# Growing the key matrix M with three products a head instead of four: two over all 128 rows with the high keys, and one for each head over 64 rows with the low keys

## The chip, the cores and the metric

The kernel runs on one core of one Trainium2 chip. The metric is the device time of one execution in microseconds (us). TensorE is PE in the profile, its weight loads PEld, VectorE DVE, ScalarE ACT, GpSimd POOL, and SyncE, which issues the DMAs, SP.

## The reference

A cross attention and a quantised linear layer, each behind a layer norm and each added to its input:

```python
def xattn(q, latent_kv, Wq, Wkv_expand, Wout):      # q: (8, 1024, 1024), latent_kv: (8, 64, 256)
    qp = q @ Wq.T
    k, v = jnp.split(latent_kv @ Wkv_expand.T, 2, axis=-1)
    # 16 heads of 64 columns: qh, kh, vh
    scores = jnp.einsum('bhqd,bhkd->bhqk', qh, kh) / jnp.sqrt(64)
    scores = jnp.where(causal, scores, jnp.finfo(scores.dtype).min)
    out = jnp.einsum('bhqk,bhkd->bhqd', softmax(scores), vh)
    return out.reshape(b, sq, H) @ Wout.T

def ffn(x, weight):                                  # weight: (1024, 1024)
    w_fp8, w_scale = quant_e4m3(weight)              # one scale for the whole tensor
    x_fp8, x_scale = quant_e4m3(x)
    return ((x_fp8 @ w_fp8.T) * (x_scale * w_scale)).astype(bfloat16)

x = x + xattn(layernorm(x), ctx, Wq, Wkv_expand, Wout)
x = x + ffn(layernorm(x), w)
```

## The kernel before

**The algebra.** There are only 64 keys a batch, so the kernel never forms the queries. For each batch it makes M, whose 64 columns for head h are Wq of that head times that head's keys, and N, which is the values times Wout. The scores of a tile of 128 rows are then x times M (1024 by 1024, 16 heads by 64 keys), and the attention's output is the probabilities times N. Each of these products is done in float16 with every number split in a high and a low part: `PASSES` lists the three part products (high by high, high by low, low by high), and `split_product` runs them over the 8 chunks of 128 rows: 8 times 3 times 2 halves of 512 columns, 48 matmuls a tile (L636).

**The order of the work.** 64 tiles, 8 a batch, 8 batches. The PE program is written out by hand: `step(b, tt, e, t)` issues the scores S of tile t+1 and then the output O of tile t. M of the next batch is grown in the seventh step of a batch (`tt == TB - 2`): two of its 8 blocks are put between chunks of S (`KEYS_AT_S`) and six between chunks of O (`KEYS_AT_O`). The N blocks are grown in pairs in the last step of a batch and in the first of the next (`make_n_pair`, L623), with matmuls on 64 rows and 64 columns of the array. The M of batch 0 is grown ahead of the first tile, each block followed by the turning of a piece of Wout (`turn_wout`, L728).

**The part that is changed.** `make_m(ct, n)` grows one block of 128 rows of M into 1024 columns of PSUM (`grow_ps`, two such buffers). `wq_stack` holds for each head, in 64 of the partitions, the high part of its weight, and in the other 64 the low part: even heads have the high part in partitions 0 to 63 (`EVEN`), odd heads in 64 to 127 (`ODD`). `k_hilo` holds the keys' high part beside the weight's high part and the low part beside the low, `k_lohi` the other way round. So two matmuls of 128 rows and 64 columns a head (L609 and L610) give all four part products, 32 matmuls a block. `place(h)` is the column block of head h in M, and so in the scores and probabilities. ACT rounds the block to its high part (`take_m`, L862) and DVE makes the low part and frees the buffer (`take_m`, L1099). `load_k` (L375) brings the keys of a batch from `kv_dram` in 8 DMAs on SP's queue, issued by `next_k` in the first step of the batch before. `got_k` counts them.

Of the kernel before, what the change touches and what calls it, by code (L numbers as in the profile page):

```python
# [25 lines left out]
F16 = mybir.dt.float16  # L26
BF16 = mybir.dt.bfloat16
U32 = mybir.dt.uint32
ALU = mybir.AluOpType
ACT = mybir.ActivationFunctionType  # L30
# [3 lines left out]
P = 128  # L34
# [7 lines left out]
N_SCALE = 2.0 ** -14  # L42
# [13 lines left out]
def xattn_ffn_kernel(nc, x, ctx, Wq, Wkv, Wout, Wffn, out):  # L56
    B, S, H = x.shape
    SK, L = ctx.shape[1:]
    NH = H // HD
    NP = NH // 2  # L60
# [11 lines left out]
    with ExitStack() as scope:  # L72
        def sb(name, shape, dt):
            return scope.enter_context(nc.sbuf_tensor(name, shape, dt))
# [9 lines left out]
        wq_stack = sb("wq_stack", [P, NH, H], F16)  # L84
        wo_t = sb("wo_t", [P, 2, NP, H], F16)
        m_buf = sb("m_buf", [P, 2, CT, H], F16)
        n_buf = sb("n_buf", [P, 2, NP, H], F16)
        k_hilo = sb("k_hilo", [P, NH, SK], F16)
        k_lohi = sb("k_lohi", [P, NH, SK], F16)
        v_rows = sb("v_rows", [P, 2, NP, SK], F16)  # L90

        w8_raw = sb("w8_raw", [P, CT, H], BF16)
# [21 lines left out]
        pt_buf = [halves(i) for i in (10, 11)]  # L114
# [39 lines left out]
        ps_s, ps_o, ps_x, ps_p = (ps_all[:, i * H:(i + 1) * H] for i in range(4))  # L154
# [20 lines left out]
        EVEN, ODD = slice(0, HD), slice(HD, P)  # L175
# [28 lines left out]
        got_k = sem("got_k")  # L204
# [19 lines left out]
        o_full = sem("o_full")  # L224
# [83 lines left out]
        QUAD = CT // 2  # L308
        grow_ps = [ps_p, ps_x]
# [9 lines left out]


        def place(h):
            return h // 4 * 4 + (0, 2, 1, 3)[h % 4]

        FIRST_PAIRS_AT = {0: 0, 3: 1, 6: 2, 8: 3}
        PAIRS_AT = {0: 1, 5: 2, 8: 3}
# [4 lines left out]
        block = scope.enter_context(nc.Block())  # L330
# [16 lines left out]
        def _(sp):  # L347
# [21 lines left out]

            def load_k(of):  # L370

                for to, swap in ((k_hilo, 0), (k_lohi, 1)):
                    for s, rows in enumerate((EVEN, ODD)):
                        for e in range(2):
                            sp.dma_start(to[rows].rearrange("d (j e) k -> d e j k", e=2)[:, e],  # L375
                                         of(s ^ swap, e)).then_inc(got_k, 16)

            def load_v(of):
                for s in range(2):
# [118 lines left out]
            for k in range(2):  # L498
                cols = slice((1 - k) * HALF, (2 - k) * HALF)
# [52 lines left out]
        def _(pe):  # L552
# [12 lines left out]
            to = next_slot()  # L565
            for lt in range(LT):
                for a in range(KEYS // P):
                    mm = nc.tensor.transpose(to[:, (lt * 4 + a) * P:(lt * 4 + a + 1) * P],
                                             ctx_f[:, a, lt * P:(lt + 1) * P], ident[:])
# [32 lines left out]
            def make_m(ct, n):  # L602
                to = grow_ps[ct % 2]
                if not is_step(n, 0):
                    pe.wait_ge(grow_free[ct % 2], n)
                for h in range(NH):
                    cols = to[:, place(h) * SK:(place(h) + 1) * SK]
                    w = wq_stack[:, h, ct * P:(ct + 1) * P]
                    nc.tensor.matmul(cols, w, k_hilo[:, h, :], start=True, stop=False)  # L609
                    mm = nc.tensor.matmul(cols, w, k_lohi[:, h, :], start=False, stop=True)  # L610
                mm.then_inc(grow_full[ct % 2], 1)


# [13 lines left out]
                                    mm.then_inc(grow_full[k], 1)  # L627


            def split_product(to, left, right, full, weave=lambda c: None, ready=lambda c: None):  # L630
                for c in range(CT):
                    ready(c)
                    for i, (ls, rs) in enumerate(PASSES):
                        for half in range(2):
                            cols = slice(half * HALF, (half + 1) * HALF)
                            mm = nc.tensor.matmul(to[:, cols], left[:, ls, c * P:(c + 1) * P], right[:, rs, c, cols],  # L636
                                                  start=(c == 0 and i == 0),
                                                  stop=(c == CT - 1 and i == len(PASSES) - 1))
                    if c == CT - 1:
                        mm.then_inc(full, 1)  # L640
                    weave(c + 1)
# [14 lines left out]
            def step(b, tt, e, t):  # L656
                known = isinstance(t, int)
                last = known and t >= T - TB
                n_here = is_step(tt, 0)
                if n_here:  # L660
                    pe.wait_ge(got_v, 32 * b + 32)
                if not known or t + 1 < T:
                    m_last = is_step(tt, TB - 1)
                    m_next = is_step(tt, TB - 2) and not last
                    pe.wait_ge(x_turned, 16 * t + 32)
                    pe.wait_ge(s_read, t + 1)
                    if m_next:
                        pe.wait_ge(got_k, 128 * b + 256)
                        if b == 2:
                            pe.wait_ge(w_scale_made, 1)  # L670
                        if b >= 3:
                            pe.wait_ge(w8_ready, 2 * (b - 2))

                    def between(c):
                        if n_here:
                            m = (FIRST_PAIRS_AT if t == 0 else PAIRS_AT).get(c)
                            if m is not None:
                                make_n_pair(b, m)
                        if m_next and c in KEYS_AT_S:
                            make_m(KEYS_AT_S[c], uses(b + 1, 0, KEYS_AT_S[c]))  # L680

                    def m_chunk(c):
                        if m_last:
                            pe.wait_ge(grow_free[c % 2], uses(b + 1, 0, c) + 1)

                    between(0)
                    split_product(ps_s, xt_buf[1 - e], m_buf, s_full, between, m_chunk)
                if last and 1 <= tt <= 4:
                    turn_w8(tt - 1)
                if b == 2 and is_step(tt, 5):  # L690
                    pe.wait_ge(w_amax_rows, 1)
                    nc.tensor.transpose(ps_x[:, 0:P], w_spread, ident[:]).then_inc(w_amax_turned, 1)
                pe.wait_ge(p_turned, 16 * t + 16)
                pe.wait_ge(x1_ready, t + 1)
                if is_step(tt, TB - 2) and not last:
                    def next_m(c):
                        for k in KEYS_AT_O.get(c, ()):
                            make_m(k, uses(b + 1, 0, k))

                    split_product(ps_o, pt_buf[e], n_buf, o_full, next_m)  # L700
                elif known and t == T - 1:
                    for half in range(2):
                        cols = slice(half * HALF, (half + 1) * HALF)
                        for c in range(CT):
                            for i, (ls, rs) in enumerate(PASSES):
                                mm = nc.tensor.matmul(ps_o[:, cols], pt_buf[e][:, ls, c * P:(c + 1) * P],  # L706
                                                      n_buf[:, rs, c, cols], start=(c == 0 and i == 0),
                                                      stop=(c == CT - 1 and i == len(PASSES) - 1))
                        mm.then_inc((o_half, o_full)[half], 1)
                else:  # L710
                    def n_chunk(c):
                        if n_here:
                            pe.wait_ge(grow_free[c % 2], uses(b, 1, c) + 1)

                    def next_n(c):
                        if is_step(tt, TB - 1) and c == NEXT_PAIR_AT:
                            pe.wait_ge(got_v, 32 * b + 64)
                            make_n_pair(b + 1, 0)

                    split_product(ps_o, pt_buf[e], n_buf, o_full, next_n, n_chunk)  # L720


            def turn_wout(j):
# [8 lines left out]
            for i in range(2):  # L732
                pe.wait_ge(got_wout[i], 16)
            turn_wout(0)
            pe.wait_ge(got_k, 128)
            for i in range(4):
                pe.wait_ge(wq_moved[i], 64)
            for c in range(CT):
# [69 lines left out]
        def _(act):  # L808
# [45 lines left out]

            def take_n(c, n):
                act.wait_ge(grow_full[c % 2], n + 1)
                nc.scalar.activation(n_buf[:, 0, c, :], grow_ps[c % 2][:], ACT.Copy,  # L857
                                     scale=N_SCALE).then_inc(grow_hi[c % 2], 1)

            def take_m(c, n):  # L860
# [165 lines left out]
            for k in range(2):  # L1026
                cols = slice((1 - k) * HALF, (2 - k) * HALF)
# [6 lines left out]
        def _(dve):  # L1034
# [45 lines left out]
            for i in range(2):  # L1080
# [3 lines left out]
                                                    in1=k_hi_t[:, part, :], op0=ALU.mult, op1=ALU.subtract)  # L1084
# [5 lines left out]

            def take_n(c, n):
                dve.wait_ge(grow_hi[c % 2], n + 1)
                nc.vector.scalar_tensor_tensor(out=n_buf[:, 1, c, :], in0=grow_ps[c % 2][:], scalar=N_SCALE,  # L1093
                                               in1=n_buf[:, 0, c, :], op0=ALU.mult,
                                               op1=ALU.subtract).then_inc(grow_free[c % 2], 1)

            def take_m(c, n):
# [233 lines left out]
            for half in range(2):  # L1331
                cols = slice(half * HALF, (half + 1) * HALF)
# [134 lines left out]
```

## Time and profile before

| | |
|---|---|
| time, median of 3 runs | 1786.26 us (1785.97 to 1786.73) |
| the profiled execution: its time | 1787.1 us |
| the profiled execution: its span, first to last instruction | 1785.3 us |
| mean granted clock of TensorE | 0.988 of full speed |
| PE busy | 1730.4 us, 97% of the span |
| DVE busy | 1327.3 us, 74% |
| ACT busy | 688.7 us, 39% |

The span falls into a start of 118 us, in which the weights are split and turned and M of batch 0 grows, the attention of 64 tiles up to about 1517 us, and the linear layer to the end. PE is busy almost all the time in the two last parts. A share of busy time counts a matmul from its start to its modelled end, so matmuls overlap in it: what one costs in a row of them is read from the distance of their starts.

### The profile page before, as it was taken

What the parts mean: (1) busy time and instruction counts of PE and PEld (TensorE: products, weight loads), DVE (VectorE), ACT (ScalarE), POOL (GpSimd) and SP (SyncE); (2) the same over time, 40 slices, a digit from 0 to 9 for tenths busy, and PEclk for the clock granted to TensorE, in tenths of its full rate; (3) what the DMA queues carried; (4) which work ended last, traced back from release to release, by engine and by line L of the source; (5) the groups of instructions that cost most, each with busy time, mean ns of one, the idle gap of its engine ahead of it and who ended that gap; (6) DMA issues with size and microseconds to landing.
All of it is one profiled execution on the core that took longest, in us unless ns stands there. A gap on an engine that the chain in (4) does not pass through costs nothing.

```text
span 1785.3 us, 25886 instructions
## 1 busy us (share of the span) xinstructions
PE 1730.4 (97%) x10457; PEld 827.7 (46%) x10482; DVE 1327.3 (74%) x1813; ACT 688.7 (39%) x643; POOL 185.4 (10%) x143
## 2 busy tenths in 40 slices
PE   8689999999999999999999999999999999799998
PEld 4434454445444544454445444544454444344444
DVE  6776778677866787778787878787878665777775
ACT  6632133223322332233223322332233221599996
POOL 0000000000000000000000000000000002155555
PEclk9799999999999999999999999999999999899999
DMA  9674555544555445554555445544553444799995
GB/s 318 155 193 119 126 116 117 131 123 119 111 138 124 110 113 133 133 109 108 132 137 114 107 127 129 129 106 120 136 124 98 119 118 101 250 318 319 319 318 181
DMA packets 404429, 272.15 MB, mean 152 GB/s; under 512 B 355056, under 2 KB 357616, under 8 KB 403824
## 3 DMA queue, kind: packets, MB, share of 16 engines
q1 hardware_dynamic: 404336, 270.84, 57.3%
q8 instruction: 66, 1.08, 0.3%
q14 instruction: 27, 0.22, 0.0%
HBM read 119.28 MB, written 71.30 MB: 107 GB/s over the span
## 4 chain that ended last, share of the span: by engine, by line
PE 91%; issue 5%; DVE 2%; ACT 1%; DMA 1%; POOL 0%; SPq 0%; POOLq 0%; DVEq 0%; ACTq 0%
PE ps_all L636 71%; PE ps_all L772 12%; PE ps_all L623 2%; PE ps_all L609 1%; PE ps_all L610 1%; PE ps_all L645 1%; PE ps_all L706 1%; PE ps_all L588 1%; DVE n_buf L1093 1%; ACT tile_space L869 0%; ACT n_buf L857 0%; DMA tile_space<-tile_space 0%; DVE amax L1072 0%; DMA tile_space<-in_ctx_dram 0%; PE ps_all L578 0%
## 5 line engine op out<-in xcount | busy, mean ns | idle before, releaser
L636 PE MATMUL ps_all<-m_buf,tile_space 128*128 128x512 f16 x3072 | 681.0, 381 | 4.8 <-DVE wo_t L1294 4.8
L636 PE MATMUL ps_all<-n_buf,tile_space 128*128 128x512 f16 x3024 | 670.1, 379 | 0.0
L636 PEld LDWEIGHTS ps_all<-m_buf,tile_space 128*128 128x128 f16 x3072 | 298.0, 98 | 368.8 <-issue 12.2
L636 PEld LDWEIGHTS ps_all<-n_buf,tile_space 128*128 128x128 f16 x3024 | 291.6, 98 | 350.6 <-issue 6.2
L883 ACT ACTIVATE tile_space<-tile_space,neg_mean 128x1024 f32<-128x1024 f32 x63 | 72.4, 1150 | 327.7 <-DVE neg_mean L1180 327.7
L527 POOL TENSOR_TENSOR rstd_x<-veps_x,minus_half 128x1 f32<-128x1 f32 x64 | 35.3, 551 | 1388.4 <-DVE veps_x L1123 1388.4
L879 ACT ACTIVATE tile_space<-tile_space,score_scale 128x1024 f32<-128x1024 f32 x64 | 73.4, 1147 | 230.6 <-DVE tile_space L1150 230.6
L875 ACT ACTIVATE tile_space<-tile_space 128x1024 f16<-128x1024 f32 x64 | 67.6, 1057 | 184.4 <-DVE tile_space L1160 184.4
L1110 DVE SCALAR_TENSOR_TENSOR tile_space<-tile_space 128x1024 f16<-128x1024 f32 x64 | 78.4, 1225 | 64.0 <-ACT tile_space L875 64.0
L772 PE MATMUL ps_all<-wo_t,tile_space 128*128 128x512 bf16 x512 | 119.9, 383 | 2.4 <-DVE tile_space L1401 1.2
L1154 DVE TENSOR_REDUCE hsum<-tile_space 128x16 f32<-128x1024 f32 x64 | 77.9, 1217 | 59.5 <-ACT tile_space L879 59.5
L1105 DVE SCALAR_TENSOR_TENSOR tile_space<-tile_space 128x1024 f16<-128x1024 f32 x64 | 78.3, 1224 | 53.9 <-ACT tile_space L869 53.9
L772 PE MATMUL ps_all<-wo_t,wq_stack 128*128 128x512 bf16 x487 | 115.4, 379 | 0.5
L869 ACT ACTIVATE tile_space<-tile_space 128x1024 f16<-128x1024 f32 x64 | 67.6, 1056 | 122.8 <-DVE tile_space L1128 122.7
L1168 DVE SCALAR_TENSOR_TENSOR tile_space<-ps_all,out_scale,tile_space 128x1024 f32<-128x1024 f32 x63 | 80.7, 1280 | 44.8 <-PE ps_all L636 44.1
L1148 DVE TENSOR_REDUCE hmax<-ps_all 128x16 f32<-128x1024 f32 x64 | 78.2, 1222 | 39.1 <-PE ps_all L636 38.8
L1099 DVE SCALAR_TENSOR_TENSOR m_buf<-ps_all,m_buf 128x1024 f16<-128x1024 f32 x64 | 78.1, 1220 | 39.0 <-ACT m_buf L862 39.0
L857 ACT ACTIVATE n_buf<-ps_all 128x1024 f16<-128x1024 f32 x64 | 63.5, 1019 | 89.7 <-PE ps_all L623 89.7
L1389 DVE SCALAR_TENSOR_TENSOR n_buf<-ps_all,n_buf 128x1024 f32<-128x1024 f32 x64 | 78.1, 1220 | 23.8 <-ACT n_buf L991 23.3
L1093 DVE SCALAR_TENSOR_TENSOR n_buf<-ps_all,n_buf 128x1024 f16<-128x1024 f32 x64 | 76.6, 1219 | 21.2 <-ACT n_buf L857 21.2
L862 ACT ACTIVATE m_buf<-ps_all 128x1024 f16<-128x1024 f32 x64 | 64.5, 1018 | 49.9 <-PE ps_all L610 49.9
L1174 DVE BATCH_NORM_STATS2 stats_b<-tile_space 128x6 f32<-128x512 f32 x126 | 81.0, 685 | 1.9
(131 smaller groups left out, 1700.7 us busy)
## 6 DMA issues: line engine op xcount, KB each, us to landing
tile_space<-in_x_dram SPq DMA_DIRECT2D x128, 512.0 KB, 3.9
x_scratch<-tile_space SPq DMA_DIRECT2D x64, 512.0 KB, 3.0
m_buf<-x_scratch SPq DMA_DIRECT2D x32, 512.0 KB, 5.6
tile_space<-x_scratch SPq DMA_DIRECT2D x32, 512.0 KB, 5.8
out_dram<-m_buf SPq DMA_DIRECT2D x32, 512.0 KB, 4.5
out_dram<-tile_space SPq DMA_DIRECT2D x31, 512.0 KB, 5.0
m_buf<-in_L_xattn_Wq_dram SPq DMA_DIRECT2D x4, 1024.0 KB, 11.1
n_buf<-in_L_xattn_Wout_dram SPq DMA_DIRECT2D x2, 2048.0 KB, 18.3
```

What stands on the lines that cost most here:

```text
L636: mm = nc.tensor.matmul(to[:, cols], left[:, ls, c * P:(c + 1) * P], right[:, rs, c, cols], start=(c == 0 and i == 0), stop=(c == CT - 1 a ...
L772: mm = nc.tensor.matmul(y_ps[e][:, cols], left[:, c * P:(c + 1) * P], w8_t[:, c, cols], start=(c == 0), stop=(c == CT - 1))
L879: nc.scalar.activation(ex, sub, ACT.Exp, scale=score_scale[:]).then_inc(exp_done, 1)
L1093: nc.vector.scalar_tensor_tensor(out=n_buf[:, 1, c, :], in0=grow_ps[c % 2][:], scalar=N_SCALE, in1=n_buf[:, 0, c, :], op0=ALU.mult, op1=AL ...
L1099: nc.vector.scalar_tensor_tensor(out=m_buf[:, 1, c, :], in0=grow_ps[c % 2][:], scalar=M_SCALE, in1=m_buf[:, 0, c, :], op0=ALU.mult, op1=AL ...
L1105: nc.vector.scalar_tensor_tensor(out=x_rows2[:, 1, :], in0=xn[e], scalar=XN_SCALE, in1=x_rows2[:, 0, :], op0=ALU.mult, op1=ALU.subtract).t ...
L1110: nc.vector.scalar_tensor_tensor(out=p_rows2[:, 1, :], in0=pr, scalar=P_SCALE, in1=p_rows2[:, 0, :], op0=ALU.mult, op1=ALU.subtract).then_ ...
L1148: nc.vector.tensor_reduce(hmax[:], heads(ps_s[:]), AX.X, ALU.max).then_inc(max_done, 1)
L1154: nc.vector.tensor_reduce(hsum[:], heads(ex), AX.X, ALU.add).then_inc(sum_done, 1)
L1168: nc.vector.scalar_tensor_tensor(out=x1[e], in0=ps_o[:], scalar=out_scale[:], in1=xr[e], op0=ALU.mult, op1=ALU.add).then_inc(x1_ready, 1)
L1174: nc.vector.bn_stats(stats_b[:, half, :], x1[e][:, half * HALF:(half + 1) * HALF]).then_inc(b_stats, 1)
L1389: nc.vector.scalar_tensor_tensor(out=a_t[e], in0=u_ps[e], scalar=ROUND_LEAST, in1=v_t[e], op0=ALU.max, op1=ALU.add).then_inc(a_done, 1)
```

## The change

`k_hilo` and `k_lohi` give way to `k_twice`, the keys' high part in both halves of the partitions for each head, and `k_low`, the low part once, even heads in partitions 0 to 63 and odd heads in 64 to 127. `make_m` takes the heads in pairs: two matmuls of 128 rows by `k_twice` (the high and the low part of the weight times the high keys), then two of 64 rows by `k_low` (the high part of the weight times the low keys), one on the upper and one on the lower half of the rows. The product of low part by low part is left out. `place` puts the even heads into the first 8 column blocks and the odd ones into the last 8, so that the two 64-row matmuls of a pair write to different halves of the PSUM buffer. `n_block` moves N's blocks to match. The keys come in 6 DMAs instead of 8.

```diff
-        k_hilo = sb("k_hilo", [P, NH, SK], F16)
-        k_lohi = sb("k_lohi", [P, NH, SK], F16)
+        k_twice = sb("k_twice", [P, NH, SK], F16)
+        k_low = sb("k_low", [P, NP, SK], F16)
...
         def place(h):
-            return h // 4 * 4 + (0, 2, 1, 3)[h % 4]
+            return h % 2 * NP + h // 2
+
+        def n_block(c):
+            return c % 2 * QUAD + c // 2
...
             def load_k(of):
 
-                for to, swap in ((k_hilo, 0), (k_lohi, 1)):
-                    for s, rows in enumerate((EVEN, ODD)):
-                        for e in range(2):
-                            sp.dma_start(to[rows].rearrange("d (j e) k -> d e j k", e=2)[:, e],
-                                         of(s ^ swap, e)).then_inc(got_k, 16)
+                for rows in (EVEN, ODD):
+                    for e in range(2):
+                        sp.dma_start(k_twice[rows].rearrange("d (j e) k -> d e j k", e=2)[:, e],
+                                     of(0, e)).then_inc(got_k, 16)
+                for e, rows in enumerate((EVEN, ODD)):
+                    sp.dma_start(k_low[rows], of(1, e)).then_inc(got_k, 16)
...
-                for h in range(NH):
-                    cols = to[:, place(h) * SK:(place(h) + 1) * SK]
-                    w = wq_stack[:, h, ct * P:(ct + 1) * P]
-                    nc.tensor.matmul(cols, w, k_hilo[:, h, :], start=True, stop=False)
-                    mm = nc.tensor.matmul(cols, w, k_lohi[:, h, :], start=False, stop=True)
+                for j in range(NP):
+                    cols = [to[:, place(h) * SK:(place(h) + 1) * SK] for h in (2 * j, 2 * j + 1)]
+                    w = [wq_stack[:, h, ct * P:(ct + 1) * P] for h in (2 * j, 2 * j + 1)]
+                    for e in range(2):
+                        nc.tensor.matmul(cols[e], w[e], k_twice[:, 2 * j + e, :], start=True, stop=False)
+                    for e, rows in enumerate((EVEN, ODD)):
+                        mm = nc.tensor.matmul(cols[e], w[e][rows], k_low[rows, j, :], start=False, stop=True)
                 mm.then_inc(grow_full[ct % 2], 1)
...
-                            mm = nc.tensor.matmul(to[:, cols], left[:, ls, c * P:(c + 1) * P], right[:, rs, c, cols],
+                            mm = nc.tensor.matmul(to[:, cols], left[:, ls, j * P:(j + 1) * P], right[:, rs, j, cols],
```

In the last hunk `j` is `n_block(c)` for O and `c` for S. `take_n` on ACT and DVE writes `n_buf[:, :, n_block(c), :]`, and the waits for `got_k` count 96 a batch instead of 128.

How PE's program changes is seen at the place in the seventh step of batch 0 where the first block of M stands between 18 and the next 18 matmuls of S. PE, before (`k_hilo` and `k_lohi` matmuls take turns, all on 128 rows, 16 times this pair in a block):

```order
L636 MATMUL ps_all<-n_buf,tile_space 128x512 x48
L636 MATMUL ps_all<-m_buf,tile_space 128x512 x18
L609 MATMUL ps_all<-k_hilo,wq_stack 128x64
L610 MATMUL ps_all<-k_lohi,wq_stack 128x64
L609 MATMUL ps_all<-k_hilo,wq_stack 128x64
```

PE, the same place now (8 times this pair of rows in a block; 128x64 is the size of the output, and the `k_low` matmuls read 64 rows):

```order
L643 MATMUL ps_all<-n_buf,tile_space 128x512 x48
L643 MATMUL ps_all<-m_buf,tile_space 128x512 x18
L614 MATMUL ps_all<-k_twice,wq_stack 128x64 x2
L616 MATMUL ps_all<-k_low,wq_stack 128x64 x2
L614 MATMUL ps_all<-k_twice,wq_stack 128x64 x2
L616 MATMUL ps_all<-k_low,wq_stack 128x64 x2
```

The number of matmuls stays at 32 a block. What changes is that after every two matmuls of 128 rows there are two of 64 rows, so that PE goes from one kind to the other 16 times a block.

SP's queue at the start of the program, before (the keys of batch 0, behind the last moves of Wq):

```order
L387 DMA wq_stack<-tile_space 64x2x1024
L375 DMA k_hilo<-tile_space 64x8x64 x4
L375 DMA k_lohi<-tile_space 64x8x64 x4
L368 DMA tile_space<-in_x_dram 128x1024 x3
```

and now:

```order
L391 DMA wq_stack<-tile_space 64x2x1024
L377 DMA k_twice<-tile_space 64x8x64 x4
L380 DMA k_low<-tile_space 64x8x64 x2
L371 DMA tile_space<-in_x_dram 128x1024 x3
```

Two DMAs fewer stand ahead of the first loads of x.

## Rows read from the trace of the kernel before

**Rows 1.** Page, busy time of each engine, and the clock in 40 slices.

```profile
PE 1730.4 (97%) x10457; PEld 827.7 (46%) x10482; DVE 1327.3 (74%) x1813; ACT 688.7 (39%) x643; POOL 185.4 (10%) x143
PEclk9799999999999999999999999999999999899999
```

**Rows 2.** Page, the chain that ended last, by line.

```profile
PE ps_all L636 71%; PE ps_all L772 12%; PE ps_all L623 2%; PE ps_all L609 1%; PE ps_all L610 1%; PE ps_all L645 1%; PE ps_all L706 1%; PE ps_all L588 1%; DVE n_buf L1093 1%; ACT tile_space L869 0%; ACT n_buf L857 0%; DMA tile_space<-tile_space 0%; DVE amax L1072 0%; DMA tile_space<-in_ctx_dram 0%; PE ps_all L578 0%
```

**Rows 3.** Windows, the attention: stretch, length, PE busy, PEclk, DMA share, GB/s.

```profile
118.00:1517.00 1399.00, 1392.82 (x8505) 1.00 0.49 121
```

**Rows 4.** Groups of instructions: busy us, mean ns of one, idle before.

```profile
L609 PE MATMUL ps_all<-k_hilo,wq_stack 128*128 128x64 f16 x1024 | 70.4, 196 | 11.9 <-DMA k_lohi<-tile_space 10.0 <-DVE m_buf L1099 1.7
L610 PE MATMUL ps_all<-k_lohi,wq_stack 128*128 128x64 f16 x1024 | 70.3, 196 | 0.0
L623 PE MATMUL ps_all<-wo_t,v_rows 64*64 64x512 f16 x768 | 49.0, 388 | 9.0 <-DVE n_buf L1093 4.9 <-issue 4.1
L862 ACT ACTIVATE m_buf<-ps_all 128x1024 f16<-128x1024 f32 x64 | 64.5, 1018 | 49.9 <-PE ps_all L610 49.9
```

**Rows 5.** Timeline of PE, first M block of batch 1: start us, us.

```profile
236.13 0.19 PE L609 MATMUL ps_all<-k_hilo,wq_stack 128*128 128x64 f16 x1
...
237.04 0.19 PE L610 MATMUL ps_all<-k_lohi,wq_stack 128*128 128x64 f16 x1
237.07 4.05 PE L636 MATMUL ps_all<-m_buf,tile_space 128*128 128x512 f16 x18
```

**Rows 6.** Chain of waits in order of time, around N pairs: start us, us.

```profile
260.60 12.95 PE ps_all L636 x60
273.55 1.42 PE ps_all L623 x24
274.97 7.88 PE ps_all L636 x36
...
284.26 6.58 PE ps_all L636 x30
```

**Rows 7.** Timeline of PE, where S or O gives way to N.

```profile
273.17 0.38 PE L636 MATMUL ps_all<-n_buf,tile_space 128*128 128x512 f16 x1
273.48 0.63 PE L623 MATMUL ps_all<-wo_t,v_rows 64*64 64x512 f16 x8
```

**Rows 8.** PE's waits over the span: us in total, times, longest.

```profile
PE ps_all L609 <- DMA k_lohi<-tile_space: 10.0, 1, 10.0
PE ps_all L623 <- DVE n_buf L1093: 4.9, 9, 1.9
PE ps_all L636 <- DVE wo_t L1294: 4.8, 1, 4.8
```

**Rows 9.** DMA issues: count, KB each, median us to landing.

```profile
k_hilo<-kv_scratch SPq DMA_DIRECT2D x28, 64.0 KB, 3.0
```

**Rows 10.** Timeline of PE, M and Wout at the start.

```profile
54.44 0.23 PE L609 MATMUL ps_all<-k_hilo,wq_stack 128*128 128x64 f16 x1 [10.04 <-DMA k_lohi<-tile_space]
...
57.67 1.07 PE L728 MATMUL ps_all<-ident,n_buf 128*128 128x128 f32 x8
...
60.03 1.09 PE L728 MATMUL ps_all<-ident,n_buf 128*128 128x128 f32 x8
```

**Rows 11.** Timeline of SP's queue at the start.

```profile
44.25 3.61 SPq L375 DMA_DIRECT2D k_hilo<-tile_space  x4
47.90 5.06 SPq L375 DMA_DIRECT2D k_lohi<-tile_space  x4
...
75.10 1.45 SPq L396 DMA_TRANSPOSE tile_space<-tile_space  x1
```

**Rows 12.** Timeline of DVE at the start, and PE's first scores.

```profile
57.56 1.23 DVE L1099 SCALAR_TENSOR_TENSOR m_buf<-ps_all,m_buf 128x1024 f16<-128x1024 f32 x1 [3.01 <-ACT m_buf L862]
...
73.86 1.22 DVE L1105 SCALAR_TENSOR_TENSOR tile_space<-tile_space 128x1024 f16<-128x1024 f32 x1
...
77.32 1.22 DVE L1099 SCALAR_TENSOR_TENSOR m_buf<-ps_all,m_buf 128x1024 f16<-128x1024 f32 x1
78.45 1.27 DVE L1294 SCALAR_TENSOR_TENSOR wo_t<-ps_all,to_f,wo_t 128x1024 f16<-128x1024 f32 x1
...
79.85 1.01 PE L636 MATMUL ps_all<-m_buf,tile_space 128*128 128x512 f16 x2 [4.76 <-DVE wo_t L1294]
```

More of the change, by code:

```diff
@@ L627, in make_n_pair, with split_product @@
                                     mm.then_inc(grow_full[k], 1)
-            def split_product(to, left, right, full, weave=lambda c: None, ready=lambda c: None):
+            def split_product(to, left, right, full, weave=lambda c: None, ready=lambda c: None, block=lambda c: c):
                 for c in range(CT):
                     ready(c)
+                    j = block(c)
                     for i, (ls, rs) in enumerate(PASSES):
@@ L667, in step @@
                     if m_next:
-                        pe.wait_ge(got_k, 128 * b + 256)
+                        pe.wait_ge(got_k, 96 * b + 192)
                         if b == 2:
@@ L698, in next_m @@
                             make_m(k, uses(b + 1, 0, k))
-                    split_product(ps_o, pt_buf[e], n_buf, o_full, next_m)
+                    split_product(ps_o, pt_buf[e], n_buf, o_full, next_m, block=n_block)
                 elif known and t == T - 1:
@@ L718, in next_n @@
                             make_n_pair(b + 1, 0)
-                    split_product(ps_o, pt_buf[e], n_buf, o_full, next_n, n_chunk)
+                    split_product(ps_o, pt_buf[e], n_buf, o_full, next_n, n_chunk, n_block)
             def turn_wout(j):
@@ L734, in _ @@
             turn_wout(0)
-            pe.wait_ge(got_k, 128)
+            pe.wait_ge(got_k, 96)
             for i in range(4):
@@ L856, in take_n @@
                 act.wait_ge(grow_full[c % 2], n + 1)
-                nc.scalar.activation(n_buf[:, 0, c, :], grow_ps[c % 2][:], ACT.Copy,
+                nc.scalar.activation(n_buf[:, 0, n_block(c), :], grow_ps[c % 2][:], ACT.Copy,
                                      scale=N_SCALE).then_inc(grow_hi[c % 2], 1)
@@ L1092, in take_n @@
                 dve.wait_ge(grow_hi[c % 2], n + 1)
-                nc.vector.scalar_tensor_tensor(out=n_buf[:, 1, c, :], in0=grow_ps[c % 2][:], scalar=N_SCALE,
-                                               in1=n_buf[:, 0, c, :], op0=ALU.mult,
+                nc.vector.scalar_tensor_tensor(out=n_buf[:, 1, n_block(c), :], in0=grow_ps[c % 2][:], scalar=N_SCALE,
+                                               in1=n_buf[:, 0, n_block(c), :], op0=ALU.mult,
                                                op1=ALU.subtract).then_inc(grow_free[c % 2], 1)
```

## The prediction

> **What bounds the kernel now.** I read the page first. PE is busy 97% of the span, at a granted clock near full speed in nearly every slice [rows 1]. The chain that ended last is PE for 91% of the span, with the products of S and O (L636) 71% and the M matmuls (L609, L610) together about 2% [rows 2]. The windows then tell where PE has no room: in the attention, 118 to 1517 us, it is busy 1392.8 of 1399 us at the full clock [rows 3]. Whatever PE does more or less in that stretch moves the end by as much, unless it is where the few microseconds of idle time lie. Its waits there are small: the N matmuls waited 4.9 us for DVE in all, over 9 places [rows 8]. So the 56 blocks of M that are grown inside the attention (8 a batch, batches 1 to 7) stand wholly on the path, and the 8 of batch 0, in the start, have to be looked at by themselves.
>
> **What an M block costs now.** The mean of 196 ns in the groups [rows 4] is the latency of one matmul and not its cost. The cost is the distance of starts: 32 matmuls start from 236.13 to 237.07 us [rows 5], 0.94 us a block, 29.3 ns each. All 56 blocks are 52.6 us of the path. That bounds any gain: of four matmul slots a pair of heads the change can save one.
>
> **What a pair of heads costs after the change.** Two matmuls of 128 rows are two slots of 29.3 ns. The two of 64 rows lie on different rows and write to different halves of the PSUM buffer, so they may run side by side. The N matmuls show that such matmuls do: 24 of them on quarters of the array, each of 512 columns, take 1.42 us [rows 6], while a full one of 512 columns takes 12.95 / 60 = 0.2158 us [rows 6]. So four run in the time of one, and the two low ones here cost one slot and some 3 ns. The streaming comes to 3 x 29.3 = 88 ns a pair instead of 117.
>
> What is added is the change from 128 rows to 64 and back, once each way a pair. The trace has that change around each N pair. Going in: the first N matmul starts at 273.48 us, the last full one before it at 273.17 [rows 7], 0.31 us where 0.216 is the rule, so 0.09 us in which nothing starts. The chain shows the whole price: the six groups of four should take 6 x 0.2158 = 1.295 us and take 1.42, 0.125 more; the 36 full matmuls behind should take 7.77 us and take 7.88, 0.11 more, and 30 behind another N pair take 6.58 where 6.47 is their sum [rows 6]. In and out is 0.235 us. About 20 ns of it is that four starts are spread at either side, where a pair of heads has two. I take 0.215 us for in and out.
>
> The Trainium skill's page "TensorEngine Tiling (Array Packing)", section Tiling Modes, says that a change of the tiling mode, unlike a change of the tile within one, drains TensorE. This rule speaks against the change, gives no price, and the 0.09 us in which nothing starts agrees with it. By the page's rule alone the sum would have the same sign and no size; the sum here goes by the rows.
>
> A pair then costs 0.088 + 0.215 = 0.303 us, where it was 0.117: 0.186 us more. A block has 8 pairs: 1.49 us more, 2.43 us instead of 0.94. The 56 blocks: **+83 us**. No row of before shows a change of rows alone, with all 128 columns kept. Its bounds: nothing at all from below, since two full matmuls of different lines follow each other without a gap (237.04 to 237.07, [rows 5]), which gives 8 x 56 x 29.3 ns = 13 us less than before; from above, each change shows the whole latency of a matmul of 64 columns that its slot does not, 196 - 29 = 167 ns [rows 4]: 0.088 + 2 x 0.167 - 0.117 = 0.305 us a pair, +137 us. I take the N pairs' price, since they are the only rows with 64-row matmuls, and they too change the rows.
>
> **The start.** Batch 0's blocks take turns with the turning of Wout: 60.03 - 57.67 = 2.36 us a round [rows 10], after the change 3.8 us. Before, DVE is what binds there: it starts at 57.56 us and has 1.2 to 1.3 us for the M block and as much for Wout, with little idle time to 79.7 us [rows 12]. With 3.8 us PE takes the lead over DVE's 2.5 us plus the norm work. Against this, the first M matmul waits until 54.44 us for the last key DMA [rows 8, 10], and 8 key DMAs took 3.61 + 5.06 us to issue [rows 11]; two fewer are 2.5 us less at the dearer rate. So PE starts at some 52 us. Two blocks before the first Wout piece cost 3.2 us (57.67 - 54.44, at a lower clock) and now at least 3 us more: the first Wout piece stands at 58.5 us instead of 57.67. The eighth block of M is then ready after 6 more rounds, 58.5 + 22.9 = 81.4 us; 1.0 us of ACT [rows 4] and 1.2 of DVE make it 83.6. Before, its part on DVE ended at 78.5 us, and the first scores started at 79.85 [rows 12], held as well by x, which DVE finished at 75.1 and SP then turned [rows 11, 12]. The first scores therefore start about 4 us later. The softmax of tile 0 hangs on them, and I pass the 4 us on in full. Bounds: 0, if the Wout work of DVE absorbs it, and 8 us, if the blocks at the lower clock pay more. **+4 us.**
>
> **Edits that cost nothing.** Key loads of batches 1 to 7: 6 DMAs instead of 8, some 3 us each to landing [rows 9]. They are issued in the first step of a batch and waited for in the seventh, over 100 us later; without that cover each would cost its 3 us. The order of N's blocks and of the columns of M moves addresses only: chunk c of O still waits for the block that was grown as c-th, and the counts and sizes on ACT and DVE are the same; one of their instructions for M takes 1.0 and 1.2 us [rows 4, 12], and longer blocks on PE give them more room, not less. At the turn of the batch the 4.9 us of waits [rows 8] may shift by a few tenths each; I put that at 0.
>
> **Sum.** 1787.1 us for the profiled execution (span 1785.3 and 1.8 around it) plus 83 and 4 is 1874 to 1875. The median of the runs shown lies 0.8 us below that execution: **1874 us**, 4.9% slower.
>
> **Rivals.**
> A. *The change of rows is free, and the two half products run side by side.* For it: 128-row matmuls of different kinds follow without a gap, and the four N matmuls of a group start within a few ns of each other. Against it: 0.31 us at every entry to N. The gain is 13 us in the attention, and the start gains perhaps 1 us of the 2.5 from the shorter key load: 1772 us. It decides at one point: in and out of a pair together must cost under 29 ns. The Trainium skill's page "TensorE: Matmul & The Clock Gate", Part 3 (Packing small matmuls), says that small products on distinct row groups run concurrently, with starts some 4 ns apart; by it alone this rival is what comes, and the trace agrees on the starts within an N group but not at its edges.
> B. *The change of rows with all columns kept costs about half as much,* because only the weights of the half rows are held back, or because only one of the two directions waits. Then a pair has 88 + 107 - 117 = 78 ns more, 35 us over 56 blocks, and the start moves by 1: 1822 us. Nothing in the rows tells which part of the N price belongs to the rows and which to the columns.
> C. *Each change shows the full latency:* +137 us, and 8 to 12 in the start: about 1933 us. Against it: 0.09 us and not 0.167 at the N pairs, although a matmul takes 0.38 us from start to modelled end there [rows 7].
> D. *The clock falls.* PE is sparsely used in an M block, and the six blocks between chunks of O make such stretches frequent. The page shows lower clock in the start, where PE idles [rows 1]. If O of that step ran at the lower of the two levels (1.2 instead of 2.4 GHz), its 48 matmuls would cost 0.216 us more each: 10 us a batch, 73 us on top, 1947 us. Against it: an M block of 2.4 us would stand between 1.3 to 3.9 us of dense work.
> E. *The two half products run one after the other:* 26 ns a pair, 12 us more: 1886 us. It lies inside the main case's range.
>
> **How the numbers follow.** Main case (with E) 0.70, A 0.10, B 0.13, C 0.04, D 0.03. The time is the main case's, 1874 us; its own range is 1850 to 1905, from the start at 0 and a change that is a fifth cheaper, to E with the start at 8 and the full 0.235 us. The range given goes down to 1812 to take in most of B, and up to 1908; A, C and D are left out. Chances: what a measurement of this kernel can tell from no change is 0.2%, 3.6 us. Faster 0.10 (A), within it 0.01, slower 0.89.
>
> **What would show it right or wrong.** In the profile after: the starts of one M block from its first `k_twice` matmul to the next L643 over 2.4 us (0.7 in A, 1.55 in B, over 3.3 in C); within a pair, about 0.12 us from the second 128-row start to the first 64-row start and about as much back, and 3 ns between the two 64-row starts (29 in E); the period of a batch at 191.6 us instead of 179.7; the granted clock at 1.00 in the seventh step (D: less); the first scores at about 84 us. The likeliest error is the price of a change of rows alone, on which 16 changes a block times 56 blocks hang: 10 ns in it are 9 us of the result.

## The result and the profile after

The changed kernel takes 1881.49 us (median of 4 runs, 1881.36 to 1881.62) where the kernel before, run beside it, took 1786.12 (1785.42 to 1786.73): a ratio of 1.0531, 95% interval 1.0518 to 1.0544, 95.4 us slower. The span of the profiled execution went from 1785.3 to 1879.7 us.

The page of the kernel after: busy time, and the chain by line.

```profile
PE 1831.8 (97%) x10482; PEld 880.1 (47%) x10482; DVE 1329.5 (71%) x1813; ACT 690.2 (37%) x643; POOL 185.6 (10%) x143
PE ps_all L643 67%; PE ps_all L779 12%; PE ps_all L614 4%; PE ps_all L616 3%; PE ps_all L629 2%; PE ps_all L652 1%; PE ps_all L713 1%; PE ps_all L592 1%; DVE n_buf L1100 1%; ACT tile_space L876 0%; ACT n_buf L864 0%; DMA tile_space<-tile_space 0%; DVE amax L1079 0%; DMA tile_space<-in_ctx_dram 0%; POOL amax_all L526 0%
```

PE is as busy in share as before, 97% [rows 1], and its busy time grew by 101 us. The M matmuls, about 2% of the span in the chain before [rows 2], are now 7% (L614 and L616). The weight loads (PEld) grew by 52 us, from 827.7 to 880.1; DVE and ACT have the same busy time within 3 us.

The groups of M's matmuls, after (busy us, mean ns of one, idle before):

```profile
L614 PE MATMUL ps_all<-k_twice,wq_stack 128*128 128x64 f16 x1024 | 121.8, 202 | 9.1 <-DMA k_low<-tile_space 9.1
L616 PE MATMUL ps_all<-k_low,wq_stack 64*128 64x64 f16 x1024 | 106.0, 203 | 0.0
```

The mean of one matmul hardly moved, from 196 to some 202 ns [rows 4]. That a block costs more shows in the busy time of the two groups together, 227.8 us where it was 140.7 [rows 4], and in the distance of the starts. Timeline of PE, the first M block of batch 1, after (start us, us):

```profile
248.01 0.38 PE L643 MATMUL ps_all<-m_buf,tile_space 128*128 128x512 f16 x1
248.23 0.22 PE L614 MATMUL ps_all<-k_twice,wq_stack 128*128 128x64 f16 x2
248.38 0.20 PE L616 MATMUL ps_all<-k_low,wq_stack 64*128 64x64 f16 x2
248.52 0.23 PE L614 MATMUL ps_all<-k_twice,wq_stack 128*128 128x64 f16 x2
...
250.49 0.20 PE L616 MATMUL ps_all<-k_low,wq_stack 64*128 64x64 f16 x2
250.62 1.25 PE L643 MATMUL ps_all<-m_buf,tile_space 128*128 128x512 f16 x5
```

From the second `k_twice` start of a pair to the first `k_low` start are 0.12 us (248.26 to 248.38; the first start of the row is 248.23 and the second 0.03 later), and about 0.13 from the second `k_low` start to the next `k_twice` start, where any two matmuls of M were 29.3 ns apart [rows 5]. A pair takes 0.300 us, the block 2.39 instead of 0.94.

The weight loads show the same break. Timeline of PEld, after:

```profile
248.02 0.31 PEld L614 LDWEIGHTS ps_all<-k_twice,wq_stack 128*128 128x128 f16 x2
248.38 0.10 PEld L616 LDWEIGHTS ps_all<-k_low,wq_stack 64*128 64x128 f16 x2
```

The first load for `k_twice` starts at 248.02, 0.21 us ahead of its matmul and while S still runs. The first load for `k_low` starts at 248.38, together with its matmul: no load of the other kind was made ahead of the change.

The chain shows what remains unchanged: 60 matmuls of S and O in 13.06 us and 36 in 7.88, as in [rows 6], with 0.11 us more on the 60 because a change of rows now stands ahead of them.

```profile
284.32 13.06 PE ps_all L643 x60
298.80 7.88 PE ps_all L643 x36
```

Where the 94.4 us of span came from is read from three marks in the traces: PE's first matmul of O, the last one of the last tile, and the end. Timelines of PE, before and after:

```profile
118.28 0.61 PE L636 MATMUL ps_all<-n_buf,tile_space 128*128 128x512 f16 x2
1528.58 1.03 PE L706 MATMUL ps_all<-n_buf,tile_space 128*128 128x512 f16 x4
```

```profile
130.38 0.60 PE L643 MATMUL ps_all<-n_buf,tile_space 128*128 128x512 f16 x2
1622.88 1.03 PE L713 MATMUL ps_all<-n_buf,tile_space 128*128 128x512 f16 x4
```

The last matmul of O is the fourth of its row, three slots of 0.216 us later: it stood at 1529.23 and stands at 1623.52. (It lies 12 us behind the 1517 us at which the section on the profile before ends the attention.) So the start has 12.1 us more, the attention 82.2, the part behind it 0.1.

### The profile page after: what moved, and what is told of

It reads as the page before. It is cut to its first block, busy times and chain, and to the rows that moved or that the text cites. A ratio compares the mean times of both kernels' runs of the same rounds, so it can differ in the third digit from the quotient of the medians.

```text
span 1879.7 us, 25895 instructions
## 1 busy us (share of the span) xinstructions
PE 1831.8 (97%) x10482; PEld 880.1 (47%) x10482; DVE 1329.5 (71%) x1813; ACT 690.2 (37%) x643; POOL 185.6 (10%) x143
## 4 chain that ended last, share of the span: by engine, by line
PE 90%; issue 5%; DVE 2%; ACT 1%; DMA 1%; POOL 0%; SPq 0%; POOLq 0%; DVEq 0%; ACTq 0%
PE ps_all L643 67%; PE ps_all L779 12%; PE ps_all L614 4%; PE ps_all L616 3%; PE ps_all L629 2%; PE ps_all L652 1%; PE ps_all L713 1%; PE ps_all L592 1%; DVE n_buf L1100 1%; ACT tile_space L876 0%; ACT n_buf L864 0%; DMA tile_space<-tile_space 0%; DVE amax L1079 0%; DMA tile_space<-in_ctx_dram 0%; POOL amax_all L526 0%
## 5 line engine op out<-in xcount | busy, mean ns | idle before, releaser
L614 PE MATMUL ps_all<-k_twice,wq_stack 128*128 128x64 f16 x1024 | 121.8, 202 | 9.1 <-DMA k_low<-tile_space 9.1
L616 PE MATMUL ps_all<-k_low,wq_stack 64*128 64x64 f16 x1024 | 106.0, 203 | 0.0
```

The lines of the kernel that those rows point to most:

```text
L614: nc.tensor.matmul(cols[e], w[e], k_twice[:, 2 * j + e, :], start=True, stop=False)
L616: mm = nc.tensor.matmul(cols[e], w[e][rows], k_low[rows, j, :], start=False, stop=True)
```

## The experiments

The theory: every change between matmuls of 128 rows and of 64 rows holds back PE's next start by about 0.106 us, 16 of them a block, and that is the loss in the attention. Rival 1: it is the order in pairs or the placing of columns. Rival 2: a 64-row matmul is dear in itself.

**fullrows: the new order and placing, all on 128 rows.**

```diff
+        k_hilo = sb("k_hilo", [P, NH, SK], F16)
+        k_lohi = sb("k_lohi", [P, NH, SK], F16)
...
+                    for k_of in (k_hilo, k_lohi):
+                        for h in heads:
+                            mm = nc.tensor.matmul(to[:, place(h) * SK:(place(h) + 1) * SK],
+                                                  wq_stack[:, h, ct * P:(ct + 1) * P], k_of[:, h, :],
+                                                  start=(k_of is k_hilo), stop=(k_of is k_lohi))
```

> The changed kernel's order of heads, placing of columns and pairs (two matmuls with the high keys, then two with the crossed keys), but all four on 128 rows as before the change, so all four part products again and 8 key DMAs. Theory (the cost is the change between 128-row and 64-row matmuls): 29 ns from start to start everywhere, an M block of 0.94 us, 1786 us in all. Rival 1 (the cost comes from the order in pairs, that is from writing the two halves of the PSUM buffer in turn): a block stays at about 2.4 us, 1881 us.

1786.73 us (ratio 1.0002, interval 0.9992 to 1.0011). Timeline of PE in its first M block of batch 1:

```profile
235.67 0.22 PE L613 MATMUL ps_all<-k_hilo,wq_stack 128*128 128x64 f16 x2
235.73 0.22 PE L613 MATMUL ps_all<-k_lohi,wq_stack 128*128 128x64 f16 x2
...
236.54 0.22 PE L613 MATMUL ps_all<-k_lohi,wq_stack 128*128 128x64 f16 x2
236.60 1.68 PE L642 MATMUL ps_all<-m_buf,tile_space 128*128 128x512 f16 x7
```

0.93 us a block. The order in pairs, the two halves of the buffer in turn, `n_block` and the crossed placing cost nothing. Rival 1 falls.

**group8: the same matmuls, 2 changes a block.**

```diff
-                for j in range(NP):
...
+                group = NP
+                for j0 in range(0, NP, group):
+                    for h in range(2 * j0, 2 * (j0 + group)):
+                        nc.tensor.matmul(to[:, place(h) * SK:(place(h) + 1) * SK], wq_stack[:, h, ct * P:(ct + 1) * P],
+                                         k_twice[:, h, :], start=(h < 2 * j0 + 2), stop=False)
+                    for h in range(2 * j0, 2 * (j0 + group)):
+                        rows = (EVEN, ODD)[h % 2]
+                        mm = nc.tensor.matmul(to[:, place(h) * SK:(place(h) + 1) * SK],
+                                              wq_stack[rows, h, ct * P:(ct + 1) * P],
+                                              k_low[rows, h // 2, :], start=False,
+                                              stop=(h >= 2 * (j0 + group) - 2))
```

> The changed kernel with all 16 matmuls of 128 rows of a block first, then its 16 of 64 rows: the same matmuls, 2 changes of rows a block instead of 16. Theory (each change costs about 0.106 us, whatever stands around it): block of 24 x 0.0293 + 2 x 0.106 = 0.92 us, attention 1.2 us shorter than before the change, start as before or up to 2 us shorter for the two DMAs fewer: 1783 to 1786 us. Rival 2 (a 64-row matmul of 64 columns is dear in itself, some 0.09 us each pair of them): no gain over the changed kernel, 1881 us.

1784.21 us (ratio 0.9985, interval 0.9976 to 0.9995); a second time 1784.52 (0.9988, 0.9979 to 0.9997). Timeline of PE, one block:

```profile
248.84 0.63 PE L613 MATMUL ps_all<-k_twice,wq_stack 128*128 128x64 f16 x16
249.40 0.41 PE L617 MATMUL ps_all<-k_low,wq_stack 64*128 64x64 f16 x16
249.74 2.12 PE L647 MATMUL ps_all<-n_buf,tile_space 128*128 128x512 f16 x9
```

0.90 us a block. The 0.34 us from 249.40 to 249.74 hold the sixteen 64-row matmuls and the way back: 8 slots of 0.029 and 0.11, so they run two at a time in one slot. The same 32 matmuls that cost 2.39 us cost 0.90, so rival 2 falls, and the saved slot, 13 us in the most hopeful case, is all but used up by the two changes that are left: a block is 0.03 us shorter than that of fullrows, some 2 us over 56 blocks. The rest of what the profiled execution gains lies in the start, where the first scores stand at 77.97 us instead of 79.85.

**group2: 8 changes a block.** The same edit with `group = 2`.

> The changed kernel with heads four at a time: four matmuls of 128 rows, then four of 64 rows, 8 changes a block. Theory: block of 24 x 0.0293 + 8 x 0.106 = 1.55 us, 0.61 us over the kernel before, 34 us in the attention, and 3 to 8 us in the start: 1823 to 1828 us. Rival 2: 1881 us. If the price of a change depended on how many matmuls stand between two of them, the block would be off the line through 16 and 2 changes.

1822.08 us (ratio 1.0202, interval 1.0185 to 1.0219). Timeline of PE, one block:

```profile
236.59 0.28 PE L613 MATMUL ps_all<-k_twice,wq_stack 128*128 128x64 f16 x4
236.81 0.23 PE L617 MATMUL ps_all<-k_low,wq_stack 64*128 64x64 f16 x4
...
237.97 0.23 PE L617 MATMUL ps_all<-k_low,wq_stack 64*128 64x64 f16 x4
238.13 2.12 PE L647 MATMUL ps_all<-m_buf,tile_space 128*128 128x512 f16 x9
```

1.54 us. Blocks with 2, 8 and 16 changes take 0.90, 1.54 and 2.39 us: 0.64 / 6 = 0.107 and 0.85 / 8 = 0.106 us a change. It is one price, whether 2, 4 or 16 matmuls stand between two changes. The time is 1 us under what was expected, since the start cost less than put down (below).

**allhalf: six 64-row matmuls a pair, none of 128.** It leaves out the product of the weight's low part and the high keys, and shows times alone.

```diff
+                    for i in range(3):
+                        for e, h in enumerate(heads):
+                            rows = (EVEN, ODD)[e]
+                            k = k_low[rows, j, :] if i == 2 else k_twice[rows, h, :]
```

> All products of an M block on 64 rows, six matmuls a pair of heads, even heads always on the upper half of the rows and odd heads on the lower. The low part of the weight by the high keys is left out, and the high part by the high keys stands in for it a second time, since a bank may be written from one half of the rows only. No change of rows within a block, 2 around it. Theory: 24 slots of two side by side, block 0.92 us, 1783 to 1786 us. Rival 2 (64-row matmuls are dear in themselves): three such slots a pair instead of one, block over 3 us, above 1900 us. A third outcome, weight loads of half the rows not side by side (six loads a pair of 29 ns): block of about 1.4 us plus 0.2, 1825 us.

1784.86 us (ratio 0.9990, interval 0.9981 to 1.0000). The timeline of PE has the start of its first M block of batch 1 at 233.58 us and the next matmul of S at 234.38:

```profile
231.75 1.89 PE L645 MATMUL ps_all<-m_buf,tile_space 128*128 128x512 f16 x8
233.58 0.23 PE L616 MATMUL ps_all<-k_twice,wq_stack 64*128 64x64 f16 x4
...
234.38 1.69 PE L645 MATMUL ps_all<-m_buf,tile_space 128*128 128x512 f16 x7
```

The last of the eight matmuls of S ahead starts at 233.26 (seven slots behind 231.75), so 0.1 us beyond its slot passes before the block. With it the block takes 0.90 us for 48 matmuls. Weight loads of half the rows are side by side too, so the third outcome falls: 64 rows are as good as 128 as long as they stay 64.

**start8 and rest8: which blocks lose how much.**

```diff
-                group = NP
+                group = NP if isinstance(n, int) and n < QUAD else 1
```

(start8; rest8 has `1 if ... else NP`.)

> Batch 0's eight M blocks with 2 changes of rows each (as in group8), all later ones with 16 (as changed). Theory (the attention's share is 56 blocks by 1.47 us = 82 us, and the rest of the loss is the start): the clock rises in the start as in group8, the first scores start at about 78 us instead of 91, 1866 to 1870 us in all. Rival (the start's delay is absorbed by the softmax of the first tile): 1878 us or more.

> The other half: batch 0's blocks with 16 changes, all later ones with 2. Theory: first scores at 91 us, clock at 0.50 of full speed up to there, 1784 + 12 to 14 = 1796 to 1798 us. The losses of this one and of start8 over group8 add up to that of the changed kernel, 97 us.

start8 1866.82 us (ratio 1.0449, interval 1.0433 to 1.0465), rest8 1798.69 (1.0068, 1.0052 to 1.0083), 0.7 us above what was expected. Over group8's 1784.21 that is 82.6 us for the 56 blocks of the attention and 14.5 for the 8 of the start, 97.1 together; the changed kernel is 97.3 over it. The two parts add up, and eight blocks in the start cost 1.8 us each against 1.48 in the attention. The windows show why. PE of start8 and of rest8 from 54 to 84 us (length, PE busy, PEclk, DMA share, GB/s):

```profile
54.00:64.00 10.00, 8.98 (x168) 0.89 0.90 338
64.00:74.00 10.00, 7.33 (x120) 0.83 0.01 3
74.00:84.00 10.00, 6.53 (x17) 0.66 0.44 106
```

```profile
54.00:64.00 10.00, 10.00 (x96) 0.50 0.97 359
64.00:74.00 10.00, 10.00 (x85) 0.50 0.00 1
74.00:84.00 10.00, 10.00 (x83) 0.50 0.01 2
```

With 16 changes a block PE reads as fully busy, and its granted clock is 0.50 throughout, the lower of the two levels (1.2 GHz). With 2 changes it is mostly at the upper in the first two windows, 0.89 and 0.83; in the third PE has only 17 matmuls, and the mean is 0.66.

**warm: does the clock stay low, or is it brought down?**

```diff
+            for i in range(96):
+                nc.tensor.matmul(grow_ps[1][:, 0:P], ident_bf[:], ident_bf[:], start=True, stop=True)
             pe.wait_ge(got_k, 96)
```

> The changed kernel with 96 more matmuls (128 columns, bfloat16) on PE in the time in which it waits for the first keys; their result is not used. Theory W (the clock stays at the lower level in the start because it is low when the M blocks begin and they never raise it): with the clock up at 53 us the blocks take 2.4 us instead of 3.0, the pieces of Wout half, first scores at 82 to 85 us, 1873 to 1876 us. Theory S (the sparse M blocks themselves bring the clock down again in the start): granted clock back at 0.50 by 60 us, 1880 to 1882 us.

1880.91 us (ratio 1.0530, interval 1.0514 to 1.0546): nothing gained. PE of warm in four windows, and its first matmul of M:

```profile
44.00:48.50 4.50, 4.50 (x82) 1.00 1.07 225
51.00:52.00 1.00, 0.00 (x0) 0.98 0.45 74
52.00:53.00 1.00, 0.08 (x2) 0.50 1.27 127
53.00:58.00 5.00, 5.00 (x54) 0.50 0.87 262
```

```profile
52.92 0.29 PE L614 MATMUL ps_all<-k_twice,wq_stack 128*128 128x64 f16 x2 [4.37 <-DMA k_low<-tile_space]
```

The added matmuls held the clock at 1.00, but they were done at about 48.5 us. PE then waited 4.37 us for the keys, and the clock fell just before 52 us, about 1 us ahead of the first block. So the clock was low again when the blocks began, as in the changed kernel, and the run doesn't decide between theory W and theory S, although its time and the 0.50 at 60 us are what theory S said. What is shown comes from start8: there too the blocks begin at the lower level, with the same wait ahead and the same pieces of Wout between them, and the clock rises (granted clock 0.50 from 52.6 to 56.1 us and 1.00 from 56.2 to 66). So 16 changes a block keep the clock down in the start. Whether they would bring it down from the upper level there, no run shows. In the attention the same blocks leave it up: the kernel after has 1.00 from 248.2 to 284 us, where they stand between chunks of S and O.

```profile
248.20:284.00 35.80, 35.80 (x333) 1.00 0.31 78
```

**two and two_b: one change less a block.** The cure for a price by the change is fewer changes.

```diff
-        KEYS_AT_S = {3: 0, 6: 1}
-        KEYS_AT_O = {1: (2,), 2: (3,), 4: (4,), 6: (5,), 7: (6,), 8: (7,)}
+        KEYS_AT_S = {4: 0}
+        KEYS_AT_O = {2: (2,), 5: (4,), 8: (6,)}
...
+                for c in cts:
+                    for h in range(NH):
+                        nc.tensor.matmul(grow_ps[c % 2][:, place(h) * SK:(place(h) + 1) * SK],
+                                         wq_stack[:, h, c * P:(c + 1) * P], k_twice[:, h, :], start=(h < 2), stop=False)
+                for c in cts:
+                    for h in range(NH):
+                        rows = (EVEN, ODD)[h % 2]
...
+                    mm.then_inc(grow_full[c % 2], 1)
```

> group8 with two blocks of M at a time in batches 1 to 7: the 32 matmuls of 128 rows of both, then their 32 of 64 rows, 2 changes of rows for two blocks; in the seventh step the first two blocks go behind chunk 4 of S, the others behind chunks 2, 5 and 8 of O. Theory: 28 times 0.21 us less than group8, 5.9 us: 1778 us. Rival (a wait for the two PSUM buffers, which both have to be free now, takes the gain): PE waits for DVE in the seventh step, 1782 us or more.

1785.90 us (ratio 0.9995, interval 0.9986 to 1.0004): the rival came. PE waits in the seventh step of a batch for the low part of M's fourth block, which stood on DVE behind the next tile's probabilities. Timeline of two, and its waits in all:

```profile
251.69 0.25 PE L613 MATMUL ps_all<-k_twice,wq_stack 128*128 128x64 f16 x3 [0.80 <-DVE m_buf L1110]
```

```profile
PE ps_all L613 <- DVE m_buf L1110: 8.0, 9, 1.7
```

By the starts the pair of blocks comes 0.96 us late, 7 times: 6.7 us, more than the 5.9 of the changes saved. two_b moves that one DVE instruction ahead:

```diff
+                if grow:
+                    grow_m(3)
                 if not known or t + 1 < T:
                     probabilities(t + 1)
-                if grow:
-                    grow_m(3)
```

> The kernel two with one change on DVE: the low part of M's fourth block is made before the probabilities of the next tile instead of behind them. In two, PE waited 0.96 us a batch for that block, at the pair of blocks behind chunk 5 of O, 7 times. If that wait took the gain of two, the wait goes away there, up to 0.5 us a batch of it may come back at the last pair of blocks (their buffer is freed about 0.4 us late), and the time is 1779 to 1782 us. If the gain of two was not there to begin with: 1785 us.

> group8 a second time, beside two_b on the same chip: 1783 to 1785 us. Where two_b stands against it tells what one change of rows in two less a block pair is worth once its wait is gone.

two_b 1778.29 us (ratio 0.9950, interval 0.9937 to 0.9964), group8 beside it 1784.52. The wait is gone from the list of PE's waits but for the one of the start:

```profile
PE ps_all L613 <- DVE m_buf L1110: 1.7, 1, 1.7
```

6.2 us between the two, where 28 changes in and out by 0.21 us were to give 5.9. In the profiled executions the stretch from the first to the last matmul of O is 1404.4 us in two_b and 1409.9 in group8, 5.5 less. group8 with DVE's new order wasn't run, so a small part of this could be the order's. two_b is faster than both kernels: 8.6 us under the one before, which took 1786.87 beside it, and 0.7 us under the range that was expected.

## Why the prediction was right, point by point

**The price of a pair of heads** was put at 0.303 us against 0.117, and is 0.300. The rows of the N pairs [rows 6, 7], though they change rows and columns at once, came close to the price of a change of rows alone: 0.235 us in and out there, 0.215 as taken, 0.212 here. At either entry nothing starts for some 0.09 us beyond the slot; the two half products start 3 ns apart, as taken. That a change of rows alone would cost nearly as much as one of rows and columns was assumed and not read from any row, and no run tests the 20 ns that were taken off; that the two prices lie within 3 ns is in part luck. The 56 blocks were put at 83 us; the attention grew by 82.2, and start8 gives 82.6. The period of a batch, put at 191.6 us, is 191.5: the chain's pieces of 60 matmuls behind M start at 284.32 us and at 475.80.

**The rivals.** A (changes are free) and B (half price) fall by the distances of the starts; C (the whole latency) too. E falls: the two 64-row starts are 3 ns apart. Of the Trainium skill's two rules, the one of "TensorEngine Tiling (Array Packing)", Tiling Modes, that a change of the mode drains the engine, agrees with what came, a price of 0.106 us a change here; that the engine is empty by then isn't shown, since the ends of matmuls are modelled in these traces. The one of "TensorE: Matmul & The Clock Gate", Part 3, that small products on distinct row groups run concurrently, holds too (3 ns between the starts), for 64-row matmuls with no change between them. Of A's most hopeful bound of 13 us, two changes a block eat 11.9 (56 x 0.212). The upper end of the main case's own range, 1905 us, doesn't come out of its terms: on 1874, 12 for E, 4 for the start at 8 and 9 for the full 0.235 us give 1899. The result doesn't hang on it.

**Edits that cost nothing**: shown as one by fullrows, which has the new placing and N's order at 1.0002 times the time before. The fewer key DMAs let PE begin at 52.84 us in the changed kernel instead of 54.44 [rows 10], 1.6 us where 2.5 were put down.

**The start is the term that was mis-sized**: +4 us, with a bound of 8, and it measured +12.1. The mechanism was right, PE taking the lead over DVE, and the size was wrong by the clock. The prediction had a round of an M block and a piece of Wout at 3.8 us, and "the first Wout piece stands at 58.5 us", with some allowance for the lower clock in the two blocks ahead of it and none behind. Timeline of PE after:

```profile
52.84 0.29 PE L614 MATMUL ps_all<-k_twice,wq_stack 128*128 128x64 f16 x2 [9.06 <-DMA k_low<-tile_space]
59.03 1.97 PE L735 MATMUL ps_all<-ident,n_buf 128*128 128x128 f32 x8
60.79 0.32 PE L614 MATMUL ps_all<-k_twice,wq_stack 128*128 128x64 f16 x2
63.91 1.97 PE L735 MATMUL ps_all<-ident,n_buf 128*128 128x128 f32 x8
90.96 1.01 PE L643 MATMUL ps_all<-m_buf,tile_space 128*128 128x512 f16 x2 [0.68 <-DVE m_buf L1106]
```

A round is 4.88 us (63.91 - 59.03). Its M block takes 3.12 us (63.91 - 60.79) where one in the attention takes 2.39, and a Wout piece 1.97 us where it was 1.09 [rows 10]. Six rounds of 1.1 us more are 6.5 us, and the first piece stands 0.5 us later than put down: with these the first scores come at 90.96 us and not at 84. The first matmul of O comes another 1.0 us late. On the way to it PE waits 6.1 us for the values (`v_rows`), where the longest wait before the change was 4.1 us; why this grew wasn't tested. The windows show the lower clock: 0.50 from 52.8 to 90.9 us in the kernel after, and 0.84 from 54.4 to 79.8 before.

```profile
52.80:90.90 38.10, 37.43 (x312) 0.50 0.39 124
```

```profile
54.40:79.80 25.40, 18.46 (x312) 0.84 0.56 175
```

Rival D, a fall of the clock, had been looked for in the attention alone, where it didn't come, and was not carried over to the start, where the same sparse blocks have no dense work around them. start8 against the changed kernel shows that the changes in the blocks keep the clock down; warm, as it came out, adds nothing to this. The total was 1874 predicted and 1881.5 measured. The start was 8.1 us dearer than put down and the attention 0.8 us cheaper, which is the 7.5 us between them to within 0.3.

## What to carry to other kernels

On PE, count the places where matmuls change between 128 rows and 64, not the matmuls: each place costs 0.106 us here, as much as 3.6 slots of a 64-column matmul, so packing two half-row products of 64 columns side by side, which saves one slot of 0.029 us, pays only when about eight such pairs stand between the change in and the change back (an estimate: 0.212 / 0.029 is 7.3; group8 has eight and gains 0.03 us a block). Sort the products by their rows over a whole block, or over two, and look then at who frees the larger buffers. Where PE's program is full of such gaps, its busy share can still read 100%: read the distance of starts and the granted clock beside it, above all in stretches without dense work around.

## What the runs showed that was not expected

A stretch in which PE reads as busy without a break (10.00 of 10.00 us) ran at half the clock: matmuls whose starts are 0.12 us apart count in the profile by their latency of 0.2 us each, and the clock, low when they began, stayed at 0.50 for the 38 us that they and the pieces of Wout took, where with 2 changes a block it rose (start8). Between dense chunks the same blocks, 2.4 us long, left the clock at 1.00. Between these two, group2's blocks of 1.54 us began at 0.50 (54 to 64 us) and had 0.96 in the next 10 us, before the dense part came:

```profile
54.00:64.00 10.00, 10.00 (x112) 0.50 0.89 333
64.00:74.00 10.00, 9.63 (x150) 0.96 0.01 2
```

With it goes that group2's start cost little (first scores at 80.3 us against 79.9 before and 91.0 after), and that the loss in the start is not in proportion to the changes as it is in the attention. What exactly decides the clock between these cases stays open.
